# Graph network kernel: coefficients from powers of Q, three coefficient products without a bias product, and new instruction orders

## What is computed

```python
# layer 0: eight Euler steps from h = x @ fc_in_w.T + fc_in_b
alph = sigmoid(alpha_train)[:, None]
w_eff = w * clip(d, 0, 1) @ w.T
for _ in range(8):
    ax = einsum('nm,bmd->bnd', adj, h)
    h = h + (1 / 8) * (alph * 0.5 * (ax - h) + h @ w_eff - h + x)
x = layernorm(x + h)
# layer 1: attention with 4 heads of 32, masked where adj == 0
q, k, v = heads(x @ W)
x = layernorm(x + softmax(q @ k.T / sqrt(32) + mask) @ v)
```

## Time and profile before

| quantity | value |
|---|---|
| median of 3 runs | 682.69 us (681.02 to 683.04) |
| profiled execution | 683.51 us |
| its span | 681.7 us |
| TensorE matmul busy | 646.5 us (95%) |
| VectorE busy | 456.5 us (67%) |
| ScalarE busy | 452.1 us (66%) |
| GpSimd busy | 72.9 us (11%) |
| mean granted TensorE clock | 0.989 |

### The profile page before, as it was taken

The page is one execution under the profiler, slowest core; times in us unless marked ns, Lnnn a source line. Parts: engine busy times, 40 slices in busy tenths (PEclk is TensorE's granted clock), DMA queues, the critical chain, the costliest instruction groups (busy, mean ns, idle before and its releaser), DMA issues.

```text
span 681.7 us, 11846 instructions
## 1 busy us (share of the span) xinstructions
PE 646.5 (95%) x3441; PEld 474.3 (70%) x3441; DVE 456.5 (67%) x1308; ACT 452.1 (66%) x1023; POOL 72.9 (11%) x86
## 2 busy tenths in 40 slices
PE   4998799999999999999999999999999999999883
PEld 3776676867777776868686777778686868676541
DVE  3442437568594958677685849485866768496986
ACT  3122146867778686868686776868686868678881
POOL 3110000001010100101010102001010101000001
PEclk9999999999999999999999999999999999999897
DMA  4000021312213130403031221303030312112211
GB/s 112 0 1 16 0 63 47 78 33 67 59 43 83 25 101 12 112 0 100 24 82 41 63 60 36 88 19 104 11 103 10 96 27 73 37 49 62 65 29 48
DMA packets 37695, 35.47 MB, mean 52 GB/s; under 512 B 7840, under 2 KB 24864, under 8 KB 37664
## 3 DMA queue, kind: packets, MB, share of 16 engines
q1 hardware_dynamic: 37664, 35.09, 20.0%
HBM read 5.57 MB, written 4.19 MB: 14 GB/s over the span
## 4 chain that ended last, share of the span: by engine, by line
PE 85%; DVE 8%; issue 3%; ACT 1%; DMA 1%; SPq 0%; POOL 0%; DVEq 0%; POOLq 0%
PE psS L711 9%; PE psO L816 8%; PE psL L697 8%; PE psL L698 8%; PE psL L699 8%; PE psE L801 7%; PE psL L689 5%; PE psL L691 5%; PE psL L690 5%; PE psM L771 4%; PE psE L797 4%; PE psL L762 2%; PE psM L776 2%; PE psS L636 2%; PE psE L636 2%
## 5 line engine op out<-in xcount | busy, mean ns | idle before, releaser
L957 DVE CUSTOM_DVE_ANT_0 Sm<-psS,mask 128x512 f32<-128x512 f32 x256 | 173.1, 687 | 109.2 <-PE psS L711 66.4
L545 ACT ACTIVATE E<-Sm,negmax 128x512 f32<-128x512 f32 x128 | 91.5, 715 | 39.7 <-DVE negmax L957 39.5
L711 PE MATMUL psS<-Ks,Qs 96*128 96x512 f32 x256 | 99.7, 447 | 4.5 <-DVE negmax L957 2.4
L545 ACT ACTIVATE Sm<-Sm,negmax 128x512 f32<-128x512 f32 x128 | 92.4, 727 | 6.6 <-DVE negmax L957 6.6
L588 ACT ACTIVATE ET<-ET 128x512 f32<-128x512 f32 x128 | 77.7, 622 | 0.4 <-DVE ET L992 0.3
L992 DVE TENSOR_TENSOR ET<-psE,maskT 128x512 f32<-128x512 f32 x120 | 77.0, 682 | 1.0 <-PE psE L797 1.0
L478 POOL TENSOR_TENSOR rstd<-var,minus_half 128x4 f32<-128x4 f32 x32 | 32.2, 1007 | 364.9 <-DVE var L940 364.9
L801 PE MATMUL psE<-ident,E 128*128 128x128 f32 x480 | 67.8, 275 | 2.3 <-ACT ET L591 1.5
L591 ACT ACTIVATE ET<-psE 128x512 f32<-128x512 f32 x116 | 68.5, 590 | 0.3 <-PE psE L801 0.3
L711 PEld LDWEIGHTS psS<-Ks,Qs 96*128 96x128 f32 x256 | 45.6, 192 | 28.7 <-issue 14.2
L801 PEld LDWEIGHTS psE<-ident,E 128*128 128x128 f32 x480 | 57.3, 142 | 8.5 <-ACT E L545 1.7
(11 more groups left out here) (158 smaller groups left out, 1100.7 us busy)
## 6 DMA issues: line engine op xcount, KB each, us to landing
Qs<-qh SPq DMA_DIRECT2D x128, 64.0 KB, 2.0
Ks<-kh SPq DMA_DIRECT2D x128, 64.0 KB, 2.0
xin<-in_x_dram SPq DMA_DIRECT2D x16, 256.0 KB, 2.9
Qs<-ql SPq DMA_DIRECT2D x64, 64.0 KB, 2.0
Ks<-kl SPq DMA_DIRECT2D x64, 64.0 KB, 2.0
out_dram<-y SPq DMA_DIRECT2D x16, 256.0 KB, 2.3
E<-in_adj_dram SPq DMA_DIRECT2D x4, 256.0 KB, 4.3
Qs<-Mh SPq DMA_DIRECT2D x16, 4.0 KB
```

Source lines behind the costliest of these rows:

```text
L545: nc.scalar.activation(row if h < TH else E[:, h % 2, i, :], row, ACT.Exp, scale=-1.0, bias=negmax[:, h * NT + i:h * NT + i + 1], accum_ou ...
L711: mm(psS[i % 2][:, :], Qs[0:KS, h, i * P:(i + 1) * P], Ks[0:KS, h, :], start=True, stop=True).then_inc(s_mm, 1)
L957: V_.tensor_tensor_reduce(out=Sm[:, i % 2, :], in0=psS[i % 2][:, :], in1=mask[:, i, :], scale=-SCALE, scalar=3e38, op0=ALU.add, op1=ALU.mi ...
```

## The change

- The recurrence is gone. Q is squared into powers by doubling: TensorE makes Q^2, Q^3 and Q^4, Q^5 to Q^8 in three products of 128, 256 and 512 columns (`q_powers`), and ScalarE copies them out. `feature_powers`, three products of 384 columns and nine of two columns, stands behind `power(1, 0)`. VectorE sums the part that comes from x in 28 scaled additions of 128x128 (`source_terms`) and adds the rest in 9 of 128x130 (`coefficient_sums`). ScalarE and VectorE split the result directly from SBUF; nine transposes fall away.
- VectorE scales the four adjacency tiles with no recurrence step between them. The DMA of alpha goes first on SyncE, those of fc_in_w and its bias behind the adjacency. GpSimd prepares other constants.
- The bias becomes one 128x512 constant `biasT`. It is worked out by three `bias_rows` of eight products each, two `bias_columns` of four small ones, one with `bcols`, and one 512-column fp32 product `bias_constant`. The first `bias_rows`, the first `bias_columns` and the `bcols` product stand in the setup, the rest in iteration 0. VectorE adds `biasT` when it evacuates J1, in place of ScalarE's copy.
- Each C block loses its product of `rb` and `Wst`.
- All tables but POOL_DRAIN are in a new order: the cut between iterations is moved, CB and S(3, 0), S(3, 1) go behind X1T and XT ahead of it, MT goes between PV2 and PV3 of the next iteration, STK of head 0 has lag 1 at the end of the table, XIN goes to its front.

```diff
 PE_EVENTS = [
...
+    ("S", 2, 0, 2), ("S", 2, 1, 2), ("PV", 0, 0, 3), ("PV", 1, 0, 3), ("PV", 2, 0, 3), ("MT", 0, 0, 2),
+    ("PV", 3, 0, 3), ("S", 2, 2, 2), ("UT", 0, 0, 1), ("Z", 1, 0, 0), ("TR", 0, 0, 2), ("TR", 0, 1, 2),
+    ("XT", 0, 0, 0), ("S", 2, 3, 2), ("X1T", 0, 0, 1), ("CB", 0, 0, 3), ("S", 3, 0, 2), ("TR", 0, 2, 2),
...
 ACT_EVENTS = [
...
+    ("TR", 3, 2, 3), ("S", 1, 3, 2), ("TR", 3, 3, 3), ("MT", 0, 0, 2), ("OT", 0, 0, 3), ("S", 2, 0, 2),
+    ("S", 2, 1, 2), ("Z", 1, 0, 0), ("X1T", 0, 0, 1), ("S", 2, 2, 2), ("S", 2, 3, 2), ("XT", 0, 0, 0),
...
 DVE_EVENTS = [
...
+    ("TR", 3, 2, 3), ("MT", 0, 0, 2), ("S", 2, 1, 2), ("LN1A", 0, 0, 1), ("TR", 3, 3, 3), ("S", 2, 2, 2),
+    ("LN1B", 0, 0, 1), ("TR", 0, 0, 2), ("S", 2, 3, 2), ("Z", 1, 0, 0), ("TR", 0, 1, 2), ("S", 3, 0, 2),
...
 SP_EVENTS = [
...
+    ("XIN", 0, 0, 0), ("STK", 1, 0, 2), ("STK", 2, 0, 2), ("OUT", 0, 0, 4), ("STK", 3, 0, 2), ("MT", 0, 0, 2),
+    ("STK", 0, 0, 1),
...
+            def q_powers(n):
+
+                pe.wait_ge(q_ev, n + 1)
+                k = 1 << n
+                mm(psM[:, 0:k * D], Qp[:, k, :], Qp[:, 1:k + 1, :], start=True, stop=True).then_inc(q_mm, 1)
+
+            def feature_powers():
+
+                pe.wait_ge(q_ev, 4)
+                pe.wait_ge(in_fc, 32)
+                pe.wait_ge(c_pool, 2)
+                for c in range(RS // 3):
+                    slots = R_BANKS[c][:, 0:3 * SLOT].rearrange("p (k s) -> p k s", s=SLOT)
+                    mm(slots[:, :, 0:D], fc[:, 0:D], Qp[:, 3 * c:3 * c + 3, :], start=True, stop=True)
+                    for k in range(3):
+                        last = mm(slots[:, k, D:SLOT], Qp[:, 3 * c + k, :], fc[:, D:SLOT], start=True, stop=True)
+                last.then_inc(r_mm, 1)
...
+            def bias_columns(q, pick):
+
+                rows = slice(q * QUAD, q * QUAD + pick.shape[0])
+                pe.wait_ge(bias_ev, (3, 7)[q])
+                n = pick.shape[1]
+                for t in range(NT):
+                    last = mm(psM[:, t * n:(t + 1) * n], wrow[rows, t * P:(t + 1) * P], pick,
+                              start=True, stop=True)
+                last.then_inc(bias_mm, 1)
+
+            def bias_rows(q):
+
+                pe.wait_ge(bias_ev, (2, 6, 9)[q])
+                for k in range(NT):
+                    for part in (PTh, PTl):
+                        last = mm(psM[0:3 * QUAD, :], wcols[q][:, k, 0:3 * QUAD], part[:, PW - 1 if q else 0, k, :],
+                                  start=k == 0 and part is PTh, stop=k == NT - 1 and part is PTl)
+                last.then_inc(bias_mm, 1)
+
+            def bias_constant():
+
+                pe.wait_ge(bias_ev, 10)
+                mm(psM[:, :], brow[:, :], wrow[:, :], start=True, stop=True).then_inc(bias_mm, 1)
...
-                if t > 0:
-                    recurrence(t - 1)
-            for m in range(NT):
+                if t < 2:
+                    q_powers(t + 1)
+            power(1, 0)
+            feature_powers()
+            for m in range(1, NT):
                 power(1, m)
-                recurrence(3 + m)
             power(2, 0)
...
+            bias_rows(0)
             power(2, 1)
...
             power(2, 2)
...
+            bias_columns(0, fold[0:PW, 0:PW - 1])
+            pe.wait_ge(bias_in, 1)
+            mm(psM[0:3 * QUAD + 1, P:P + D], bcols[:, :], ident[:, :], start=True, stop=True).then_inc(bias_mm, 1)
             power(2, 3)
...
-                mm(bank, rb[0:3 * QUAD, block, :], Wst[0:3 * QUAD, :], start=True, stop=False)
...
-                    mm(bank, Rh[:, k, :], zh[:, i, :], start=False, stop=False)
+                    mm(bank, Rh[:, k, :], zh[:, i, :], start=i == 0, stop=False)
...
+                    if isinstance(g, int) and g == 0 and j == 0:
+                        if (kind, n) == ("YT", 0):
+                            pe.wait_ge(pt_lo, PW * NT)
+                            bias_rows(1)
+                        elif (kind, n) == ("J", 0):
+                            bias_columns(1, fold[QUAD:QUAD + 2 * PW, :])
+                        elif (kind, n) == ("YT", 1):
+                            bias_rows(2)
...
+            def source_terms(first, last):
+                for n in range(first, last):
+                    m, k = TERMS[n]
+                    before = [q for q, term in enumerate(TERMS[:n]) if term[1] == k]
+                    dve.wait_ge(v_done, 1 + STEPS + (before[-1] + 1 if before else 0))
+                    V_.scalar_tensor_tensor(out=Rf[:, k, 0:D], in0=Qp[:, m, :], scalar=DT * math.comb(m + k, k),
+                                            in1=Rf[:, k, 0:D], op0=ALU.mult, op1=ALU.add).then_inc(v_done, 1)
+
+            def coefficient_sums():
+                dve.wait_ge(r_mm, 1)
+                dve.wait_ge(v_done, 1 + STEPS + len(TERMS))
+                for k in range(RS):
+                    power_of_q = STEPS - k
+                    src = R_BANKS[power_of_q // 3][:, power_of_q % 3 * SLOT:(power_of_q % 3 + 1) * SLOT]
+                    V_.scalar_tensor_tensor(out=Rf[:, k, :], in0=src, scalar=float(BINOMIAL[k]), in1=Rf[:, k, :],
+                                            op0=ALU.mult, op1=ALU.add).then_inc(r_ev, 1)
...
+                    elif kind == "J":
+                        dve.wait_ge(l0_mm, l0_unit(b, (kind, n)) + 1)
+                        bank = L0_BANK[L0_UNITS.index((kind, n))]
+                        V_.tensor_tensor(YT[:, :], psL[bank][:, :], biasT[:, :], ALU.add).then_inc(l0_ev[bank], 1)
```

250 lines of the change are left out of this document (129 added, 121 removed), and 118 rows, old and new, of tables (ACT_DRAIN, ACT_EVENTS, DVE_DRAIN, DVE_EVENTS).

## The result

The changed kernel takes **693.2 us** (median of 4 runs, 692.0 to 694.3) against 682.9 for the kernel before beside it (4 runs, 681.0 to 684.9): a ratio of 1.015, with a 95% interval from 1.011 to 1.019. It is slower by 1.5%. The forecast was 671.2 with a range of 664.5 to 678.0, so sign and size are wrong. The profiled execution took 692.1, 1.8 more than its span.

The account below looks back on a forecast made before the run. TensorE bounds the loop (busy 39.84 of 40 us), with setup and iterations 0 and 1 costed apart. Terms -11.2 + 2.8 - 2.5 - 3.8 + 2.2 + 1.0 = -11.5 gave 672.0 profiled, 671.2 median; range 664.5 to 678.

Parts of the forecast that it names:

- Loop, the new orders: Loop tables: X1T loses cover and waits 0.2 us more per graph over 14 graphs, +2.8; bounds 0 and +7.
- Iteration 1: VectorE's J1 evacuation pushes mask ahead of LN1A, 1.35 later; XT takes 0.36 back: +1.0, bounds 0 and +2.
- L684: C blocks: the dropped product of rb and Wst, 48 times at 0.23 us, saves 11.2 us.
- Setup: Start to first Z1: tiles made in a row save 2.5 us, the new powers 3.8; forecast -6.3.
- the powers: Setup from power(1, 0) to first Z1: new products and waits sum to 8.55 for 12.3, -3.8; bounds -6 and -1.
- The wait of `bias_rows(0)`: Setup: TensorE waits 0.4 us for VectorE's nine coefficient_sums and two more instructions.
- The dear end for small VectorE instructions: Setup: small VectorE instructions cost 0.35 us each instead of 0.25, making the time 0.9 higher.
- Iteration 0: Two bias_rows in existing waits, four small products and bias_constant add 2.2 us; bounds +1 and +4.
- Drain: Same events with small swaps, costed at nothing, from -2 to +2.
- Rival 3: Loop orders wait more than they free: 0.5 more per graph, 7 us, giving 678.2; chance 0.10.
- Rival 4: Slower: MT holds VectorE ahead of LN1A, delaying X1T; at 1.2 per graph, 685.2; chance 0.07.
- rival 1: Loop gains all: new order waits no more at X1T than the old, 668.4; chance 0.17.

Follow-up runs that it names:

- xs_late: Changed kernel with ScalarE's XS moved five events back, behind J(0) and two more score tiles: 689.3 us, ratio 1.006.
- xs_late_keep: xs_late with GpSimd's KEEP also put ahead of LN2A's root: 685.8 us, ratio 1.003.
- xs_early_cover: Changed kernel with XS ahead of YT(0), Xl ahead of LN2A's root, X1T behind CB and S(3, 0): 682.8 us, ratio 0.998.
- the last pair: Two kernels with moves on TensorE alone: products of one kind parted in old_order, 684.0 us, and joined in xs_early_cover, 703.3 us.
- new_masks: Changed kernel with only the masks split: mask ahead of iteration 0's YT(0) evacuation, maskT tiles behind LN1A and LN1B: 691.1 us, ratio 1.010.
- old_order: Changed kernel with the event tables of before, only J1 moved to VectorE's table: 673.0 us, ratio 0.982.
- before: The kernel before the change, unaltered: 682.9 us, ratio 1.
- before_contend: Kernel before with XS two events later and KEEP behind LN2A's root, so that Xl falls on LN2B: 684.8 us, ratio 1.000.
- mask_late: Changed kernel with all of mask and maskT put behind the moments of LN1A of graph 0: 696.3 us, ratio 1.017.

## Why the prediction was wrong

**The step that failed is "Loop, the new orders"**, sized at +2.8. With the new arithmetic under the old tables and under the new ones, the orders cost 19.2 us between UT of graph 1 and of graph 15. That step looked only for waits of TensorE on a releaser that comes late by the durations of before. Two things were missing in it. First, it went through VectorE's events with their old durations and never asked what GpSimd does beside them. Moving `XS` and `KEEP` laid GpSimd's copies on LN2B, which went from 1.11 to 2.31, and the score maxima right behind it held TensorE: taking both away gives 0.66 per period, 7.9 us over the 14 (`xs_late`, `xs_late_keep`). Second, the other 11.3 us can be named only in part. X1T's cover and the earlier `XS` give 3.1 more; the 8.2 that are left after these repairs (`xs_early_cover` against the old orders, 0.58 per graph) show no named wait. What makes them up stays open: the last pair changed the kinds and the waits together.

**"Iteration 1"**, +1.0, was right in its mechanism and wrong in its price. LN1A came behind the masks, and the wait at X1T is 3.30 as forecast. But I priced the wait by its length alone. With the pause, TensorE's granted clock fell to 0.63 to 0.69, and the products behind it took 2.75 more. A smaller part is XT: it was to take 0.36 back by standing ahead of X1T, but the first Q product waits for ScalarE's copy of X1T and comes 1.35 behind X1T where it came 1.31, so UT to Q is 1.4 longer and not 1.0. Net of L684, iteration 1 lost 4.3 where 1.0 was forecast; `new_masks` gives 4.9 back. The 2.75 are those of this execution: with the same wait `xs_late` paid about half.

**The other steps held.** L684: 11.2 was forecast for 48 products, 0.69 per graph (48 x 0.23 is 11.0, a slip of 0.2). With the old orders the steady period fell by 0.56, and 14 periods by 8.6 where 9.7 was forecast; J1 on VectorE may hold the rest, which no run parted. Setup: -6.3 forecast, -6.5 in this execution, though others with the same setup have some 2 us less of it. Of its parts, `power(1, 0)` came at 14.74 instead of 15.2, 3.0 earlier where 2.5 was forecast, and the powers gave 3.5 for 3.8. In them the wait of `power(2, 0)` was 0.73 instead of 0.85, and `feature_powers` took 3.86 for 3.9. The wait of `bias_rows(0)` was 0.5 dearer, with the cast of 1.35 ahead of it, and the 0.5 set aside for a slow TensorE was not needed in this execution; that the two cancel is luck. The dear end for small VectorE instructions, 0.35 apiece, did not come true: they start 0.2 us apart. Iteration 0: +1.86, where +2.2 less 0.7 for L684 makes +1.5. Drain: -1.0, inside the bounds. With the new orders taken out, the kernel is `old_order`, and its ratio, times 682.7, gives 670.5, where the forecast without its +2.8 for the orders is 668.4. Its profiled execution lies behind the forecast by 1.9 in the setup (first Z1 at 48.65), 1.8 in iteration 1 and 1.1 in L684's term of the loop.

**The rivals.** Rival 3 named the right place (several small waits) at 0.5 more per graph; it was 1.2 more. Rival 4 was on the right side by the wrong mechanism: MT did not delay LN1A, since X1T's chain is as short as forecast (4.98 from UT). The range (whose lower end should be 664.7 by the prediction's own bounds, 3.7 below rival 1) left out both, because I let the loop's orders cost 7 us at most. That bound came from the one wait that I had found. Nothing in the profile bounded those I had not found.

## What to carry to other kernels

Price an order change as a change of its own, apart from the arithmetic that comes with it: running the new arithmetic with the old tables takes one run, and here it turned 1.5% slower into 1.8% faster. When a copy on GpSimd moves, look at what VectorE does in SBUF in that very stretch, and then at what stands behind that instruction: the same 1 us cost 0.07 of a period in one order and several tenths in the other. A wait of TensorE can cost more than its length (here 0.95 more of waiting came with 2.75 us lost behind it), so a few one-time instructions of VectorE (here the masks) are worth splitting around the chain that TensorE waits for.

## What the hardware showed that I had not expected

- One `tensor_scalar` of 128 x 128 from SBUF to SBUF takes 0.34 us, and 1.33 to 1.34 when GpSimd's subtraction of 128 x 512 (1.28 to 1.35) starts beside it; the same tile beside GpSimd's copy of 128 x 512 (0.61) takes 0.53 at most. A cast of 128 x 4 lasted 1.35 beside a memset of 1.81. Score maxima, `Yl` and the moments of LN2A beside the same copies kept their 0.68, 0.69 and 0.87.
- In iteration 1 TensorE's granted clock stayed at 1.00 behind waits of 1.17, 1.59 and 1.61 and fell behind every one of 3.27 to 3.74; behind 2.35 it stayed up in `before` and fell in `before_contend`. In the setup it fell behind 1.87, and behind 2.85 it stayed up in the changed kernel and fell in `mask_late`. So the length of the last pause alone does not decide it.
- A single score product mostly costs TensorE 0.32 to the next start of another kind (0.23 ahead of some), and two together 0.46 to 0.56.
